# Attention block on one core: inverse sums on 16 columns, context scaling on VectorE, the merge transfer issued ahead of the next head's sum

## What is computed

```python
xn = _layernorm(x)                                  # x: (4, 2048, 512), f32
q = split_heads(xn @ q_w.T + q_b, 16) / sqrt(32)    # 16 heads of 32
k = split_heads(xn @ k_w.T + k_b, 16)
v = split_heads(xn @ v_w.T + v_b, 16)
attn = softmax(einsum('bhqd,bhkd->bhqk', q, k))
ctx = einsum('bhqk,bhkd->bhqd', attn, v)
h = xn @ weight @ aux_weight1 @ aux_weight2
return x + (merge_heads(ctx) @ out_w.T + out_b) + tanh(h + bias)
```

## Time and profile before

| | |
|---|---|
| median of 3 runs | 4139.67 us (4138.31 to 4141.12) |
| profiled execution: its time | 4140.99 us |
| profiled execution: its span | 4139.2 us, granted TensorE clock 0.995 |
| busy over the span | PE 98%, POOL 79%, DVE 76%, PEld 60%, ACT 57% |
| transfers issued by POOL | 50.2% of 16 DMA engines' span |

### The profile page before, as it was taken

How to read it: one execution, slowest core, us unless ns; L and a number is a source line. 1 busy time by engine, 2 the same in 40 slices (tenths; PEclk the granted TensorE clock), 3 DMA queues, 4 the chain that set the end, 5 groups by cost and what they waited for, 6 DMA issues and landing times.

```text
span 4139.2 us, 77715 instructions
## 1 busy us (share of the span) xinstructions
PE 4072.0 (98%) x21216; PEld 2495.7 (60%) x21216; DVE 3125.5 (76%) x5058; ACT 2356.7 (57%) x4515; POOL 3253.4 (79%) x1180
## 2 busy tenths in 40 slices
PE   8999999999999999999999999999999999999999
PEld 6888888755555555555555555555555555555467
DVE  4344334788888888888888888888888888888554
ACT  2222222266666666766666667666666766676621
POOL 1222222299999999999999999999999999999930
PEclk9999999999999999999999999999999999999999
DMA  4444445578888888888888887888888888888787
GB/s 170 158 167 162 152 147 169 161 149 175 174 178 172 174 170 175 170 173 176 176 176 172 174 170 167 175 175 175 179 169 176 172 173 172 176 176 173 156 263 262
DMA packets 246352, 722.11 MB, mean 174 GB/s; under 512 B 87392, under 2 KB 88416, under 8 KB 184544
## 3 DMA queue, kind: packets, MB, share of 16 engines
q0 software_dynamic: 55296, 402.68, 50.2%
q1 hardware_dynamic: 107648, 201.88, 14.4%
q10 hardware_dynamic: 83040, 113.01, 9.8%
HBM read 178.00 MB, written 136.31 MB: 76 GB/s over the span
## 4 chain that ended last, share of the span: by engine, by line
PE 46%; DMA 19%; issue 9%; POOL 3%; ACT 3%; POOLq 0%; ACTq 0%; SPq 0%; DVE 0%; DVEq 0%
PE sm_bank L1015 14%; PE pv_bank L1037 14%; PE st_bank L1031 14%; DMA dma_sum<-probs 11%; DMA dma_sum<-pool_sum 8%; ACT probs L846 3%; PE sm_bank L261 2%; POOL pool_sum L781 2%; PE sm_bank L1037 1%; PE st_bank L261 1%; POOL ctx_out L806 1%; PE sm_bank L1024 0%; POOL dma_sum L792 0%; DMA q_stack<-s_ctx 0%; ACTq L845 0%
## 5 line engine op out<-in xcount | busy, mean ns | idle before, releaser
L929 DVE TENSOR_REDUCE part_max<-sm_bank 128x1 f32<-128x512 f32 x4016 | 2442.1, 678 | 410.9 <-PE sm_bank L1015 404.1
L781 POOL TENSOR_TENSOR pool_sum<-pool_sum,probs 128x2048 f32<-128x2048 f32 x512 | 2504.8, 4892 | 16.6 <-ACT probs L846 0.7
L846 ACT ACTIVATE probs<-st_bank 128x512 f32<-128x512 f32 x3840 | 1959.8, 616 | 611.9 <-PE st_bank L1031 585.5
L1031 PE MATMUL st_bank<-q_stack,k_stack 97*128 97x512 f32 x4096 | 1649.2, 404 | 15.0 <-ACT probs L846 8.5
L1015 PE MATMUL sm_bank<-k_stack,q_stack 96*128 96x512 f32 x4016 | 1655.5, 412 | 5.3 <-issue 2.8
L1015 PEld LDWEIGHTS sm_bank<-k_stack,q_stack 96*128 96x128 f32 x4016 | 764.8, 190 | 551.9 <-DVE part_max L929 331.7
L1031 PEld LDWEIGHTS st_bank<-q_stack,k_stack 97*128 97x128 f32 x4096 | 780.5, 191 | 268.4 <-ACT probs L846 127.5
L1037 PE MATMUL pv_bank<-probs,v_pairs 128*32 128x512 f32 x7680 | 934.9, 602 | 0.0
L1037 PEld LDWEIGHTS pv_bank<-probs,v_pairs 128*32 128x32 f32 x7680 | 205.5, 110 | 455.7 <-ACT probs L846 262.8
L792 POOL DMA_DIRECT2D dma_sum<-probs x320 | 348.6, 1089 | 66.0 <-ACT probs L846 28.9
L405 POOL TENSOR_TENSOR y_out<-y_out,x_in 128x512 f32<-128x512 f32 x64 | 82.8, 1293 | 369.6 <-ACT y_out L437 365.2
(11 more groups left out here) (116 smaller groups left out, 3198.6 us busy)
## 6 DMA issues: line engine op xcount, KB each, us to landing
dma_sum<-probs POOLq DMA_DIRECT2D x320, 1024.0 KB, 8.3
dma_sum<-pool_sum POOLq DMA_DIRECT2D x64, 1024.0 KB, 10.2
q_stack<-s_q_hi ACTq DMA_DIRECT2D x122, 256.0 KB, 6.4
k_stack<-s_k_hi ACTq DMA_DIRECT2D x122, 256.0 KB, 4.4
x_in<-in_x SPq DMA_DIRECT2D x16, 1024.0 KB, 7.7
s_q_hi<-qk_hi SPq DMA_DIRECT2D x16, 1024.0 KB, 4.3
s_q_lo<-qk_lo SPq DMA_DIRECT2D x16, 1024.0 KB, 6.4
s_k_hi<-qk_hi SPq DMA_DIRECT2D x16, 1024.0 KB, 4.3
```

The lines of the kernel that those rows point to most:

```text
L781: nc.gpsimd.tensor_tensor(total[:], one[:], tile_at(r, kt)[:], ALU.add).then_inc(pool_added, 1)
L846: nc.scalar.activation(tile_at(r, kt)[:, q * BLK:(q + 1) * BLK], st_bank[:, st_place(kt * QB + q)], ACT.Exp, scale=SCALE).then_inc(probs_r ...
L929: nc.vector.tensor_reduce(part_max[:, k:k + 1], sm_bank[:, sm_place(k)], AX.X, ALU.max).then_inc(max_scores_read, 1)
L1031: nc.tensor.matmul(st_bank[:, st_place(u)], k_st[r][0:ROWS + 1, kt * P:(kt + 1) * P], q_st[r][0:ROWS + 1, q * BLK:(q + 1) * BLK], start=Tr ...
```

## The change

1. The `ones` become 1/32. DVE sums the sum bank over groups of 32 columns with a block transpose (`invert`), which gives 16 totals per partition, takes the reciprocal of these 16 columns, and spreads them with a 32x32 block transpose of a broadcast (`spread_out`). ACT's copy of the sums and DVE's three reciprocals of 168, 168 and 176 columns are gone.
2. `scale` moves from POOL to DVE, behind unit 15 of the maxima.
3. POOL's `merge` of a head stands directly behind its ninth add, ahead of join 1 and add 0 of the next head.
4. The two skipped score slots move from units 22 and 44 to units 24 and 48, which are the first units behind a `use`.

```diff
+ST_SKIPS = (24, 48)
 SUM_UNIT = 56
-RECIPS = [63, 7, 15]
+INVERT, SPREAD, SCALED = SUM_UNIT, 63, 15
...
-MERGE_AFTER = 0
...
-SCALE_ADD = 8
...
-    return u + (u >= 22) + (u >= 44)
+    return u + sum(u >= skip for skip in ST_SKIPS)
...
-            nc.gpsimd.memset(keep["ones"][:], 1.0)
+            nc.gpsimd.memset(keep["ones"][:], 1.0 / DH)
...
-            def scale(h, r):
-                pool.wait_ge(pv_copied, PRIME + h + 1)
-                pool.wait_ge(recip_ready, h * len(RECIPS) + len(RECIPS))
-                pool.wait_ge(context_stored[r % 2], PRIME + (h // 2) * (CTX_DMAS * DMA))
-                nc.gpsimd.tensor_tensor(ctx_out[r % 2][:], pv_copy[r % 2][:], ratio[:], ALU.mult).then_inc(context_ready, 1)
...
             def body(h, r, more, following):
+                merge(h, r)
                 for i in range(POOL_ADDS):
-                    if i == SCALE_ADD:
-                        scale(h, r)
                     if more >= 1:
                         sum_up(following, (r + 1) % GROUP, i)
-                    if i == MERGE_AFTER:
-                        merge(h, r)
...
-                        if kt == CUT - 1:
-                            copy_sums(h, r)
...
+            def invert(h):
+                dve.wait_ge(sums_ready, PRIME + h + 1)
+                nc.vector.tensor_reduce(totals[:], sum_bank.rearrange("p (b j) -> p b j", j=DH), AX.X, ALU.add,
+                                        apply_transpose=True).then_inc(sums_turned, 1)
+                dve.wait_ge(sums_turned, PRIME + h + 1)
+                nc.vector.reciprocal(inverse[:], totals[:]).then_inc(inverse_ready, 1)
+
+            def spread_out(h):
+                dve.wait_ge(inverse_ready, h + 1)
+                nc.vector.transpose(ratio[:].rearrange("p (b j) -> p b j", j=DH),
+                                    inverse[:].unsqueeze(2).to_broadcast([P, BLK // DH, DH])).then_inc(ratio_ready, 1)
+
+            def scale(h, r):
+                dve.wait_ge(pv_copied, PRIME + h + 1)
+                dve.wait_ge(ratio_ready, h + 1)
+                dve.wait_ge(context_stored[r % 2], PRIME + (h // 2) * (CTX_DMAS * DMA))
+                nc.vector.tensor_tensor(ctx_out[r % 2][:], pv_copy[r % 2][:], ratio[:], ALU.mult).then_inc(context_ready, 1)
...
-                    pe.wait_ge(sums_copied, PRIME + s - 1)
+                    pe.wait_ge(sums_turned, PRIME + s - 1)
```

More of the change, by code:

```diff
@@ L111 @@
 assert early_maxima(BLOCKS - 1, BLOCK_UNITS - 1)[-1] == HEAD_MAXIMA - 1 and UNITS < TURN_SLOT
+assert all(skip % (2 * PER_TILE) == 0 for skip in ST_SKIPS)
 assert UNITS == 64 and len(SM_TURN) % SM_BANKS == 0 and st_slot(UNITS - 1) == 65
@@ L624, in build_attend @@
         pv_copy = [sb(f"pv_copy{s}", [P, BLK]) for s in range(2)]
-        sum_copy = [sb(f"sum_copy{s}", [P, BLK]) for s in range(2)]
+        totals, inverse = sb("totals", [P, BLK // DH]), sb("inverse", [P, BLK // DH])
         ratio = sb("ratio", [P, BLK])
@@ L639, in build_attend @@
         join_due, joined = sem("join_due"), [sem("joined0"), sem("joined1")]
-        pool_added, sums_ready, recip_ready, context_ready = sem("pool_added"), sem("sums_ready"), sem("recip_ready"), sem("context_ready")
-        pv_copied, sums_copied = sem("pv_copied"), sem("sums_copied")
+        pool_added, sums_ready, context_ready = sem("pool_added"), sem("sums_ready"), sem("context_ready")
+        pv_copied, sums_turned = sem("pv_copied"), sem("sums_turned")
+        inverse_ready, ratio_ready = sem("inverse_ready"), sem("ratio_ready")
         context_stored = [sem("context_stored0"), sem("context_stored1")]
@@ L767, in _ @@
             pool.sem_inc(pool_added, PRIME)
-            pool.sem_inc(context_ready, PRIME)
             nc.gpsimd.memset(k_st[3][MROW:MROW + 1, :].bitcast(F32), 1.0).then_inc(consts_ready, 1)
@@ L830, in _ @@
         def _(act):
-            for s in (probs_ready, pv_copied, sums_copied):
+            for s in (probs_ready, pv_copied):
                 act.sem_inc(s, PRIME)
@@ L848, in exps, with copy_pv @@
                                          scale=SCALE).then_inc(probs_ready, 1)
-            def copy_bank(h, r, bank, copies, ready, value, copied):
-                act.wait_ge(ready, value)
+            def copy_pv(h, r):
+                act.wait_ge(tile_used, PRIME + h * KT + KT)
                 act.wait_ge(context_ready, PRIME + h - 1)
[L853 to L859, removed]
+                nc.scalar.activation(pv_copy[r % 2][:], pv_bank[:], ACT.Copy).then_inc(pv_copied, 1)
             def high(n, par):
@@ L907, in _ @@
             dve.sem_inc(row_max_ready, PRIME + 1)
+            dve.sem_inc(sums_turned, PRIME)
+            dve.sem_inc(context_ready, PRIME)
             def negate(s):
@@ L912, in negate @@
                                         ALU.mult).then_inc(max_row_ready, 1)
[L914 to L921, removed]
+            def invert(h):
[13 more added lines that the diff above has]
+                nc.vector.tensor_tensor(ctx_out[r % 2][:], pv_copy[r % 2][:], ratio[:], ALU.mult).then_inc(context_ready, 1)
             def maxima(s, k, units, sums_of):
+                if k == INVERT and sums_of is not None:
+                    invert(sums_of[0])
                 if units:
@@ L930, in maxima @@
                                             ALU.max).then_inc(max_scores_read, 1)
-                if k in RECIPS and sums_of is not None:
-                    recip(*sums_of, RECIPS.index(k))
+                if k == SPREAD and sums_of is not None:
+                    spread_out(sums_of[0])
+                if k == SCALED and sums_of is not None:
+                    scale(*sums_of)
             def begin(s, units=True, new=True, sums_of=None):
@@ L981, in body @@
                     results(1, 1)
-                    for piece in range(len(RECIPS)):
-                        recip(h, r, piece)
+                    invert(h)
+                    spread_out(h)
+                    scale(h, r)
                 else:
```

## The result

The changed kernel takes 4399.76 us in the median of 4 runs (4397.34 to 4416.06), the kernel before 4140.4 beside it; the ratio is 1.0634 with a 95% interval of 1.0608 to 1.0661. The forecast was 4405.

A forecast was written before the change was run, and what follows sets the result against it. POOL was taken as the bound: stretches of 8.0, 0.7, 13.8 and 30.4 us sum to 52.9 a head against 48.7, adding 265 us to 4141, so 4406, forecast 4405 for the median; range 4240 to 4520.

The forecast's parts named there:

- The bound and the sum: POOL's program over one head sets the time: 52.9 us against 48.7, 4.2 more in 63 heads, 265 us.
- join 1' to join 2': POOL stretch: 9.7 us of own work, but join 2' waits for join 1' to land behind the merge, 13.8 us.
- Most observations named in advance: Profile signs: join 1 landing 12 to 15 us, waits before merge and join 2, POOL's share near 90%, longer DVE product.
- The wait ahead of the merge: On POOL, before each merge: a wait of nearly 3 us for join 5's landing.
- PE's idle time: PE idle several us a head at tile 9's scores, none at the sums' matmul.
- Join 5 to merge: POOL stretch: issue and one add are 5.2 us, but the merge waits for join 5's landing and starts at 8.0.
- Product off POOL "gains nothing": The 1.25 us taken off POOL with the scale lie within its 2.8 us wait for join 5's landing.
- The product's hold on POOL: DVE's product may hold POOL up to 0.7 us a head, 44 us in all; taken as 0.
- The exclusion: DVE's two-SBUF-input product waits up to one POOL add, 4.5 us; covered while PE has 5.3 us to spare.
- 4.0 a head: Delay of DVE's product against the old reciprocal, costing PE where uncovered; as the deciding bound 4324 us, chance 0.10.
- The gap of 6.5 us between the landings: Merge and join 1' land 6.5 us apart, taken near the smaller observed gap; 5.4 and 8.6 give the range.
- Inverse and bank skips "at most 69 us, if PE decided": Bank skips and earlier merge save PE 1.1 us a head, at most 69 us; PE was forecast not to decide.

The follow-up runs named there:

- merge_back: The changed kernel with the merge put back behind the first add of the next head: 4294.5 us, ratio 1.0368 to the kernel before.
- no_product: The late-merge form of the changed kernel, its DVE product replaced by a same-size block transpose with one SBUF input, division left out: 4088.4 us (0.9879).
- inverse_and_skips: The kernel before with the 16-column inverse and new bank skips; product on POOL and merge where they were: 4156.3 us (1.0036).
- scale_on_pool: The changed kernel with the product back on POOL, ahead of its ninth add, and the merge still early: 4470.9 us (1.0798).
- early_merge_alone: The kernel before with the merge ahead of the loop of adds as its only change: 4473.1 us (1.0794).
- later_loads: scale_on_pool with the first two loads of a coming head two tiles later and the next two one tile later: 4393.4 us (1.0610).

## Why the prediction was right, point by point

**The bound and the sum: right.** 52.94 us a head against 52.9, and 4.14 more than before in 63 heads is 261 us; measured 259. The largest term, join 1' to join 2', was 13.33 for 13.8. Most observations named in advance are there: join 1 lands 12.5 us behind its issue, join 2 waits for that (3.12 us in the mean), joins 3 to 5 don't wait, POOL's share is down to 89%, and the product is well above 0.69. The wait ahead of the merge was 2.26 us in the mean where nearly 3 was forecast. Join 1' waited, too, for 0.24 us, which is over half of what made 1.09 of the 0.7 from the merge to it.

**PE's idle time: in another place.** The prediction put several us a head at tile 9's scores. PE was idle for 49 us in the 1000 of the window, 2.6 a head, and the waits over the whole span show most of it as waits for DVE's maxima (between 1000 and 3600 us 43 such waits of over 0.4 us, each right behind a product):

```profile
PE sm_bank L1013 <- DVE part_max L924: 122.4, 55, 3.8
...
PE st_bank L1029 <- ACT probs L837: 62.5, 29, 6.9
```

**Join 5 to merge: size right (7.76 for 8.0), floor wrong.** The prediction took 5.2 us as what POOL needs there and 2.8 as the wait for the landing. It left out that the merge waits for its own add as well. With join 5 small and the product on POOL the stretch is 7.51; less the product's 1.25 that is 6.3. The landing is thus worth some 1.5 us, and the add's completion about 1.

**Product off POOL "gains nothing": nearly.** 8.18 us with it, 7.76 without. 0.4 us.

**The product's hold on POOL: taken as 0, bound 0.7.** The stretch from join 4' to join 5' shows it: 10.41 against 10.14. It is 0.27 us a head, 17 us in all.

**The exclusion: right, and right that it was covered in this kernel.** It takes 3.77 us of DVE a head. The row that it was read from the earlier trace rows is a subtraction and not a product, with two SBUF inputs all the same. Where the cover is gone it costs 206 us (merge_back less no_product); 138 are left of these against inverse_and_skips, since POOL no longer has the 1.25 us of the product. The "4.0 a head" for PE was high: merge_back's 51.21 less no_product's 47.91 is 3.3.

**What it missed: the parts don't add, and part of the fit is luck.** The gap of 6.5 us between the landings was picked between 5.4 and 8.6, for loads that run in the same stretch, but not by when they start. In the changed kernel the two landings are 6.5 us apart in the mean, in scale_on_pool 7.6, in early_merge_alone 7.4, and in later_loads 6.0. The same sum would have put the early merge alone at about 265 us, and it lost 332. That the gap came down to the forecast's size goes with the later loads, which the prediction didn't see coming.

**Inverse and bank skips "at most 69 us, if PE decided": nothing.** inverse_and_skips has 48.85 us a head in its profile against 48.80, and its runs are 0.4% slower. POOL is busy for 980 us of the 1000 in both. DVE's lighter work (838 and not 867) and PE's (981 and not 988) went into idle time, as they do where POOL decides. No run parts the inverse from the skips. Why its other nine runs (4147 to 4166) lie above the profiled one (4141) stays open. The forms that the trace lacked took 0.72, 0.25 and 0.70 us (0.65, 0.2 and 0.65 taken).

## What to carry to other kernels

When a transfer is moved, count what is left between it and the transfer that it waits for, and what is left between it and the next in its queue: both shrank below a landing time here, and POOL stood for the rest. Waits count on the engine that is full 98% of the time; here work saved elsewhere brought nothing. When the profile names one releaser for a wait with several conditions, compare the start with each of them over many heads. A product of two SBUF tiles on VectorE beside long GpSimd adds waited for the running add; with one operand in PSUM it didn't, which turned 3.55 us into 0.69, and merge_back's ratio of 1.0368 into 0.9963.

## What the runs showed of the hardware

- VectorE beside GpSimd's adds of 128x2048: two SBUF inputs 3.77 us in the changed kernel (0.68 to 5.77) and 3.55 in merge_back, one SBUF input and one PSUM bank 0.69, one SBUF input 0.70, for 512 columns. In merge_back all 51 with two ended 0.56 us behind the end of the add in which they started.
- A GpSimd DMA that needs the add directly ahead of it starts 0.71 us behind that add's end, 5.58 behind its start; the next instruction otherwise starts 4.54 behind the start.
- Behind a 2.16 us wait of TensorE the granted clock was 0.98 over 2.5 us, 0.53 over the next 3.5, then 1.00. 16 matmuls took 3.51 us there and not 1.92.
- A transfer issued by GpSimd that waited for another one to land started 0.57 us behind that landing (join 2, 48 of 48 heads).
- Two 1 MB accumulating transfers issued 0.8 to 1.4 us apart: the second landed 12.5 or 14.1 us behind its issue, depending on when two 256 KB loads beside it started, against 7.0 for join 5 with no other join in flight.
